# Centring six chunks from the high and low float32r parts of their input

## What is computed

```python
# layer 0
x = layernorm(pair, ln1_w, ln1_b)
left = sigmoid(x @ left1) * (x @ left2)
right = sigmoid(x @ right1) * (x @ right2)
p = layernorm(einsum('nsre,nkre->nske', left, right), ln2_w, ln2_b)
x1 = pair + einsum('nrse,ez->nsrz', p, out_w) * sigmoid(x @ gate)
# layer 1
left = x1 @ W_left + b_left + (x1 @ W_eq + b_eq)
right_sum = sum(x1 @ W_right + b_right, axis=2)
out = left * right_sum * sigmoid(x1 @ W_gate + b_gate)
result = layernorm(out @ W_out + b_out + x1, ln_scale, ln_bias)
```

## Time and profile before

| what | value |
|---|---|
| median of 3 runs | 106.36 us (106.17 to 106.42) |
| the profiled execution | 106.18 us, of which the profile's span is 104.4 us |
| PE (TensorE matmuls) busy | 88.4 us, 85% |
| PEld (weight loads, beside PE) busy | 68.0 us, 65% |
| DVE busy | 76.4 us, 73% |
| ACT busy | 65.8 us, 63% |
| POOL busy | 59.7 us, 57% |
| mean granted TensorE clock | 0.961 of full speed |

### The profile page before, as it was taken

The page is one execution under the profiler, slowest core; times in us unless marked ns, Lnnn a source line. Parts: engine busy times, 40 slices in busy tenths (PEclk is TensorE's granted clock), DMA queues, the critical chain, the costliest instruction groups (busy, mean ns, idle before and its releaser), DMA issues. The chain is left out here.

```text
span 104.4 us, 1824 instructions
## 1 busy us (share of the span) xinstructions
PE 88.4 (85%) x564; PEld 68.0 (65%) x564; DVE 76.4 (73%) x284; ACT 65.8 (63%) x107; POOL 59.7 (57%) x75
## 2 busy tenths in 40 slices
PE   0998679989999799999999799999989999973100
PEld 0995468867777699845445577877877978843000
DVE  0476599986777920098996768966799999898850
ACT  0623978987776246687569945499566936865300
POOL 5128985799960010005560949549999970699500
PEclk9999999999999999999999999999999999999555
DMA  3999995000000000000000000000042048009895
GB/s 53 191 153 147 146 146 60 0 0 0 0 0 0 3 6 0 0 0 0 0 3 0 6 3 0 0 0 0 0 73 34 0 68 133 0 2 146 135 141 81
DMA packets 33545, 4.52 MB, mean 43 GB/s; under 512 B 33408, under 2 KB 33536, under 8 KB 33536
## 3 DMA queue, kind: packets, MB, share of 16 engines
q1 hardware_dynamic: 31776, 4.03, 30.8%
q10 hardware_dynamic: 1760, 0.38, 2.0%
HBM read 2.31 MB, written 2.10 MB: 42 GB/s over the span
## 5 line engine op out<-in xcount | busy, mean ns | idle before, releaser
L638 DVE TENSOR_TENSOR lr<-bank,sig_lr 128x512 f32<-128x512 f32 x16 | 15.9, 1046 | 3.9 <-ACT sig_lr L458 3.9
L355 POOL TENSOR_TENSOR t_tok<-p_sb,rstd 128x512 f32<-128x512 f32 x7 | 10.1, 1445 | 12.9 <-DVE rstd L708 12.9
L893 PE MATMUL bank<-lr_blk,xnT 64*128 64x256 f32 x128 | 16.3, 390 | 0.8 <-ACT xnT L448 0.7
L893 PEld LDWEIGHTS bank<-lr_blk,xnT 64*128 64x128 f32 x128 | 11.7, 186 | 3.5 <-issue 1.5
L702 DVE BATCH_NORM_STATS2 stats<-p_sb 128x6 f32<-128x64 f32 x64 | 8.5, 211 | 7.0 <-ACT p_sb L492 7.0
L458 ACT ACTIVATE sig_lr<-bank 128x512 f32<-128x512 f32 x16 | 9.6, 598 | 3.9 <-PE bank L893 3.9
L363 POOL TENSOR_TENSOR x_low<-x1T,x_high 128x512 fp32r<-128x512 f32 x6 | 7.7, 1287 | 5.9 <-ACT x_high L528 5.9
L371 POOL TENSOR_TENSOR oT<-o_a,rsum 128x512 f32<-128x512 f32 x8 | 8.8, 1094 | 4.1 <-DVE o_a L749 3.1
L1076 PE MATMUL bank<-wout_blk,oT 128*128 128x128 f32 x64 | 9.0, 285 | 2.3 <-POOL oT L371 2.3
L1076 PEld LDWEIGHTS bank<-wout_blk,oT 128*128 128x128 f32 x64 | 8.3, 197 | 4.0 <-POOL oT L371 2.5
L739 DVE SCALAR_TENSOR_TENSOR x1T<-bank,w_rep,u 128x128 f32<-128x128 f32 x32 | 9.2, 345 | 0.7 <-PE bank L1076 0.5
(11 more groups left out here) (102 smaller groups left out, 189.3 us busy)
## 6 DMA issues: line engine op xcount, KB each, us to landing
x_tok<-in_x SPq DMA_DIRECT2D x14, 128.0 KB, 4.3
out<-sq SPq DMA_DIRECT2D x7, 256.0 KB, 3.3
x_tok<-in_x SPq DMA_DIRECT2D x3, 64.0 KB, 3.0
w_rep<-in_weights ACTq DMA_DIRECT2D x4, 45.1 KB, 3.1
out<-sq ACTq DMA_DIRECT2D x1, 128.0 KB, 3.1
out<-sq SPq DMA_DIRECT2D x1, 128.0 KB, 3.3
x_tok<-in_x ACTq DMA_DIRECT2D x1, 64.0 KB, 2.6
row_rep<-in_rows SPq DMA_DIRECT2D x1, 32.0 KB, 3.8
```

Of the source, the lines that this page charges most:

```text
L355: nc.gpsimd.tensor_tensor(place(t_tok[:, c % 2], 0, SPC), even_first(p_sb[:, :, s]), even_first(rstd[:, 1:2, s]).to_broadcast([P, 2, SPC / ...
L638: nc.vector.tensor_tensor(lr[:, :, s].rearrange("p f s -> p s f"), src[:, :, 2 * CH:4 * CH], sig_lr[:, j % 3].rearrange("p (s f) -> p s f" ...
L893: last = nc.tensor.matmul(dst, xnT[half, c, k * P:(k + 1) * P], lr_blk[half].rearrange("p g m c -> p g (m c)"), start=True, stop=True, ski ...
```

## The change

Chunks 1 to 6 take the mean off x1 with two float32r matmuls per block in place of one float32 matmul: one on `x1_high`, one on `x1_low`, both with `centre_exact`, a float32r copy of the centring matrix that POOL makes once. Chunks 0 and 7 stay as they were. Since `x1_high` and `x1_low` of chunk c are now read until the centring has ended, the last matmul of it signals a new semaphore `cy_ps`, and `high1` and `low1` wait for the centring of chunk c - 2, whose buffer they overwrite. In the changed kernel line numbers are larger by 6 behind `low1`, by 8 behind `high1` and by 20 behind `centre_y` (L437 is L443, L528 is L536, L535 is L543, L1017 is L1025, L1076 is L1096; L1065 is L1078, L1080 and L1083).

```diff
+        centre_exact = sb("centre_exact", [P, P], fp32r)
...
+        centre_exact_ready, cy_ps = sem("centre_exact_ready"), sem("cy_ps")
...
             for n, blk in enumerate((leq_blk, gate1_blk)):
                 nc.gpsimd.tensor_copy(proj_high[:, n], blk[:]).then_inc(proj_split, 1)
+            pool.wait_ge(centre_ready, 1)
+            nc.gpsimd.tensor_copy(centre_exact[:], centre_blk[:]).then_inc(centre_exact_ready, 1)
             pool.wait_ge(proj_split, 2)
...
                 pool.wait_ge(x1_high_ready, SPLIT.index(c) + 1)
                 if c >= 2:
                     pool.wait_ge(l_ps, c - 1)
+                if c - 2 in SPLIT:
+                    pool.wait_ge(cy_ps, SPLIT.index(c - 2) + 1)
                 nc.gpsimd.tensor_tensor(x1_low[:, c % 2], x1T[:, c % 3], x1_high[:, c % 2],
                                         ALU.subtract).then_inc(x1_low_ready, 1)
...
                 act.wait_ge(x1_ready, BLK * (c + 1))
                 if c >= 2:
                     act.wait_ge(l_ps, c - 1)
+                if c - 2 in SPLIT:
+                    act.wait_ge(cy_ps, SPLIT.index(c - 2) + 1)
                 nc.scalar.activation(x1_high[:, c % 2], x1T[:, c % 3], ACT.Copy).then_inc(x1_high_ready, 1)
...
                 pe.wait_ge(x1_ready, BLK * (c + 1))
+                if c in SPLIT:
+                    pe.wait_ge(centre_exact_ready, 1)
+                    pe.wait_ge(x1_low_ready, SPLIT.index(c) + 1)
                 for j in range(BLK):
                     k = slice(j * P, (j + 1) * P)
-                    nc.tensor.matmul(in_order(bank[:, b], j), x1T[:, c % 3, k], centre_blk[:], start=j == 0, stop=False,
-                                     skip_group_check=True)
+                    if c in SPLIT:
+
+                        nc.tensor.matmul(in_order(bank[:, b], j), x1_high[:, c % 2, k], centre_exact[:],
+                                         start=j == 0, stop=False, skip_group_check=True)
+                        last = nc.tensor.matmul(in_order(bank[:, b], j), x1_low[:, c % 2, k], centre_exact[:],
+                                                start=False, stop=False, skip_group_check=True)
+                    else:
+                        nc.tensor.matmul(in_order(bank[:, b], j), x1T[:, c % 3, k], centre_blk[:], start=j == 0,
+                                         stop=False, skip_group_check=True)
+                if c in SPLIT:
+                    last.then_inc(cy_ps, 1)
```

## The result

The changed kernel took **108.53 us** (median of 4 executions, 107.67 to 109.26) beside 106.39 us (4 executions, 106.17 to 106.54): a ratio of 1.0206, with an interval of 1.0128 to 1.0283. It is slower; whether by 2% the interval leaves open. The forecast was 108.1 us in a range of 107.1 to 109.1.

What follows compares the result with a forecast made beforehand. It took PE and DVE, both full from 76 to 88 us, as the bound, with `gated1(6)` deciding. Terms 0.0, 0.0, 0.0 and 1.8 on 106.18 gave 107.98, by the median 108.16; forecast 108.1 us, range 107.1 to 109.1.

Steps and rivals of the forecast that it cites:

- Edit 1: Centring on PE: eight float32r records replace eight float32 ones at 0.111 us each, worth 0.0 us.
- Rivals A and B: Float32r matmul of 128 columns: A, cheap at 0.058 us, 107.1, chance 0.20; B, dear, 108.9 or 113.7, chance 0.08.
- Edit 2: POOL's third cast, the copy of the centring matrix: covered by idle time, worth 0.0 us, without cover 0.29 once.
- Edit 3: PE's waits for `centre_exact_ready` and `x1_low_ready`: `left_low(c)` ahead already waited for the same semaphore value, worth 0.0 us.
- Edit 4: Wait of `high1(c)` on ACT for the centring of chunk c - 2: the deciding part, worth +1.8 us.
- The wait is missed by 2.3 us: On ACT `high1(5)` ran at 76.20, but `centre_y(3)` on PE ends at 78.46, 2.3 us later.
- `gate1(4)` and `gated1(4)` 1.9 later: ACT's `gate1(4)`, queued behind `high1(5)`, and DVE's `gated1(4)`, which waits for it, each start 1.9 us later.
- `gated1(6)` 1.8 later: DVE's queue has no gap and 0.08 us of slack, so `gated1(6)` and the chain to the end move by 1.8 us.
- Which path leads: Before `gated1(6)`, DVE is ready at 90.2, PE's `left_low(6)` ends near 89.4; DVE leads and 1.8 us stands.
- nothing is added: POOL's `low1` has the same wait but stands behind `high1` of the same chunk, so it adds no delay.
- Rival C: PE's relief outruns the wait: at 0.058 us a record six centrings save PE 2.5 us; 105.9 us, chance 0.03.
- Rival D: The wait is met anyway: the delay of `high1(5)` vanishes in gaps, time stays at 106.2 to 106.4 us; chance 0.04.

Runs made afterwards that it cites:

- Experiment 2: The changed kernel with three buffers for `x1_high` and `x1_low`, so copies wait for the centring of chunk c - 3: 106.41 us beside 106.55, ratio 0.9981.
- experiment 3: The kernel before with only the third cast on POOL added, its result read by nobody: 106.38 us beside 106.55, ratio 0.9974.
- experiment 8: Two unused matmuls filling PE's gap ahead of the triangle product: kernel before 106.26 us, changed kernel 107.89, changed kernel with three buffers 106.40.
- Experiments 4 to 6: Changed kernel with `gate1(4)` and `root3_of(1)` ahead of `high1(5)`: 108.03 us; only `gate1(4)` ahead: 107.78; that plus POOL's `times_right(4)` ahead of `low1(5)`: 107.59.

## Why the prediction was right

**Edit 1, the matmuls: right.** I put the new record at 0.111 us, between 0.058 and 0.23. The starts in `centre_y(3)` are 0.112 us apart; the weight loads, the reason for the choice, are still 192 ns long by the form of the changed kernel's PEld:

```profile
L1080 PEld LDWEIGHTS bank<-centre_exact,x_low 128*128 128x128 f32 x24 | 4.6, 192 | 0.0
```

Experiment 2 puts the worth of all six centrings at zero. Rivals A and B fall with it. The Trainium skill ("TensorE: Matmul & The Clock Gate", section "Back-to-back issue gap"), by whose 81 ns for 128 columns A would have given 107.5 to 107.7, is not borne out for these matmuls: 112 ns stand here, and the measurement decides. **Edit 2: right** (experiment 3; in the trace the cast is 0.29 us, as the two before it). **Edit 3: right:** the first record of `centre_y(3)` follows the sums on PE, and among the waits of PE there is none at L1078 or L1080.

**Edit 4, the wait: right in its steps, 0.3 us too large in its sum.**

- The wait is missed by 2.3 us: 80.12 less 1.6, against 76.20, is 2.3.
- `gate1(4)` and `gated1(4)` 1.9 later: 80.66 and 81.42 less 1.6 are 1.9 each.
- `gated1(6)` 1.8 later: here the term was mis-sized, it is 1.55 to 1.58. I wrote that DVE's queue has no gap and 0.08 us of slack. From `o_a` of chunk 4 to that of chunk 6 it took 10.44 us before (88.37 - 77.93) and 10.11 after (91.53 - 81.42). 0.16 of these 0.33 us are the gap itself: I let the reading of 0.08 us at 88.21 end before `o_a` may start, while in the trace after a reading and `o_a` start together, at 91.53. The rest are small steps, the largest of 0.08 us just ahead of `o_a` of chunk 5.
- The end: `o_a` of chunk 6 carries its 1.55 us whole up to `project_y(7)`, which starts at 98.68 (95.51 before). Behind it stand two differences that I did not have and that nearly cancel. The eight records took 1.17 us, and before, in its chain:

```profile
95.51 1.53 PE bank L1076 x8
```

In the kernel before the granted clock was 0.99 from 95.51 to 96.16 us and 0.50 from there to 97.04: it fell to the level of 1.2 GHz in the midst of them. In the changed kernel it was 1.00 throughout. That gives 0.36 us back. But the last transfer to `out` took longer from issue to landing, 3.3 us before and 3.6 after, by the two pages:

```profile
out<-sq SPq DMA_DIRECT2D x1, 128.0 KB, 3.3
out<-sq SPq DMA_DIRECT2D x1, 128.0 KB, 3.6
```

Together 1.5 us are left, and over the executions with the gap filled the difference is 1.5 us too.

**Which path leads: right, but by less than I wrote.** I had DVE ready 0.8 us behind PE's `left_low(6)` (90.2 against 89.4). POOL's `low1(6)` took 1.70 us where I counted 1.29, which the runs don't explain, and `left_low(6)` ended at 91.37 (POOL's timeline, then PE's):

```profile
86.77 1.70 POOL L369 TENSOR_TENSOR x_low<-x1T,x_high 128x512 fp32r<-128x512 f32 x1
...
90.98 0.39 PE L1025 MATMUL bank<-x_low,proj_high 128*128 128x512 f32 x1
```

Less 1.6 that is 89.8, and DVE starts `o_a` at 89.9: it led by 0.16 us only.

With 1.5 in place of 1.8, the forecast would have been 107.9, what experiment 8 measured. That the median of the first four was 108.53 is the lowered clock in two of them, which the prediction did not foresee; it should have listed a stretch at 1.2 GHz among the things that can add 1.6 us to an execution. That this median still lies in the range is in part luck: with three such executions of four it would have been 109.25, above 109.1.

**One sentence was too narrow.** I followed `gate1(4)` as the path, and POOL's `low1` only as "nothing is added"; `std` was followed as waiting for DVE. Experiments 4 to 6 show that the late copy can cost by three ways: the gate behind it, ACT's list behind it (`std`), and POOL's `low1(5)`, which feeds PE. In the changed kernel the first is the longest: there `std` waits 0.17 us for DVE, and POOL 0.91 us for `o_a`. For the time it made no difference; for whoever would mend it by turning a list, it does.

**Rival C** asked for 1.3 us of slack on DVE: 0.33 was there. Even with half of the centring's matmuls gone (and no wait) the gain was 0.4 us. **Rival D** asked for gaps to swallow the delay: ACT's idle time is there in full.

## What to carry to other kernels

A new reader of a double buffer is a new wait of the writer: find where the last reader of the buffer before last stands in its engine's list, and compare its end with the start of the next write. Here it ended 2.3 us too late, and the operation behind the writer on its in-order queue paid, however cheap the new matmuls were; a third buffer takes all of it away, a turn of the order about half at best. And ask of a late operation not only what stands behind it, but all that reads it: where there are three ways, mending one shows the next.

## What was not expected of the hardware

- After some 0.54 us of waiting in front of a run of matmuls, PE's granted clock fell to 0.50 for about 3.4 us in the three profiled executions that were long (1.6 us lost), and stayed at 1.00 behind the same wait in others. Long executions were 14 of 65 with the gap, and 0 of 28 with two matmuls in it that nothing reads.
- A float32r matmul of 128 columns costs what one of the two records of a float32 matmul does, 0.111 us in a stream where each has a weight load of its own. High and low part together cost what plain float32 did, so splitting buys no time here.
- At the end, where PE idles 2.29 us ahead of the last eight records in the kernel before, the granted clock falls to 0.50 in every profile, and these records take 1.17 us if it falls behind them, 1.25 to 1.72 if in their midst (1.53 in the kernel before), 2.09 if ahead of them (experiments 4 and 5). But the last transfer to `out` then takes 3.6, 3.5 to 3.2, and 2.9 us: over the twelve profiles records and transfer together are 4.7 to 5.0 us. So the place of the fall hardly shows in the time; why the transfer makes up for it, the runs don't show.
